# A decoder's first self-attention layer: merging its weighted values by DMA through DRAM instead of by transposes on TensorE

## The reference

```python
def proj(w, b):
    y = jnp.einsum('bsd,ed->bse', x, w) + b
    return y.reshape(B, S, N_HEADS, HEAD_DIM).transpose(0, 2, 1, 3)
q = rope(proj(wq, bq)); k = rope(proj(wk, bk)); v = proj(wv, bv)
score = jnp.einsum('bhqd,bhkd->bhqk', q, k) / math.sqrt(HEAD_DIM)
score = jnp.where(causal[None, None], score, -jnp.inf)
attn = jax.nn.softmax(score, axis=-1)
out = jnp.einsum('bhqk,bhkd->bhqd', attn, v)
out = out.transpose(0, 2, 1, 3).reshape(B, S, DIM)
return jnp.einsum('bsd,ed->bse', out, wo) + bo
```

## Time and profile before

| | |
|---|---|
| Median of three executions | 828.93 us (827.77 to 837.93) |
| The profiled execution | 833.08 us, its span 831.0 us |
| Mean granted TensorE clock | 0.898 |
| TensorE busy over the span | 677.5 us (82%) |
| DVE, ACT, POOL busy | 589.4, 413.5, 284.0 us |
| Moved by DMA | 71.27 MB, mean 86 GB/s |
| Chain that ended last, by engine | PE 60%, DVE 18%, issue 8%, POOL 5%, ACT 4%, DMA 4% |

### The profile page before, as it was taken

One profiled execution on the slowest core, in us unless ns is written; L12 is line 12 of the kernel. 1 busy time (PEld: TensorE's weight loads), 2 busy tenths in 40 slices (PEclk: granted clock), 3 DMA queues, 4 the chain that ended last, 5 costly groups with the idle time before them and its releaser, 6 DMA issues.

```text
span 831.0 us, 14947 instructions
## 1 busy us (share of the span) xinstructions
PE 677.5 (82%) x4693; PEld 330.3 (40%) x4698; DVE 589.4 (71%) x1606; ACT 413.5 (50%) x708; POOL 284.0 (34%) x504
## 2 busy tenths in 40 slices
PE   2759999999988885099999933687999989897987
PEld 1335454444445443056666622122332323323543
DVE  3757778777647776567878845688889898953564
ACT  1332565655666552023333312156788777785544
POOL 4742454445542146612323210213232142341310
PEclk9875999999989987589999985578999999999899
DMA  7452655484232315211111133221224111000000
GB/s 222 148 182 99 203 160 164 123 230 141 84 87 73 99 44 166 71 36 40 42 43 40 42 112 108 73 85 44 82 73 128 31 48 52 2 2 1 13 14 26
DMA packets 74780, 71.27 MB, mean 86 GB/s; under 512 B 14560, under 2 KB 67168, under 8 KB 74704
## 3 DMA queue, kind: packets, MB, share of 16 engines
q1 hardware_dynamic: 72000, 64.84, 25.9%
q0 software_dynamic: 2272, 4.69, 1.8%
q10 hardware_dynamic: 432, 0.79, 0.3%
HBM read 41.90 MB, written 28.00 MB: 84 GB/s over the span
## 4 chain that ended last, share of the span: by engine, by line
PE 60%; DVE 18%; issue 8%; POOL 5%; ACT 4%; DMA 4%; SPq 1%; DVEq 0%; POOLq 0%; ACTq 0%
PE bank_pv L733 10%; DVE mx L591 9%; PE bank_turn L575 8%; PE bank_scores L2025 5%; PE bank_scores L1775 4%; PE bank_turn L1760 4%; PE bank_scores L685 4%; PE bank_scores L1760 4%; POOL routed_tokens L1727 2%; PE bank_turn L752 2%; PE bank_scores L1768 2%; PE bank_turn L528 1%; DMA stk<-stack_A 1%; PE bank_turn L579 1%; DVE stats L450 1%
## 5 line engine op out<-in xcount | busy, mean ns | idle before, releaser
L591 DVE TENSOR_REDUCE mx<-bank_turn 128x1 f32<-128x512 f32 (+3 forms) x452 | 260.7, 616 | 63.2 <-PE bank_turn L580 33.3
L575 PE MATMUL bank_turn<-stk 64*128 64x128 bf16 (+3 forms) x708 | 167.0, 318 | 29.4 <-DVE mx L591 19.8
L685 PE MATMUL bank_scores<-stk 64*128 64x512 bf16 (+4 forms) x576 | 173.6, 364 | 4.6 <-ACT probs L706 3.6
L710 ACT ACTIVATE probs<-bank_scores 128x1024 f32<-128x1024 f32 (+4 forms) x160 | 117.3, 768 | 102.9 <-PE bank_scores L685 102.5
L706 ACT ACTIVATE probs<-bank_scores 128x512 f32<-128x512 f32 x256 | 138.6, 606 | 35.7 <-PE bank_scores L685 34.7
L733 PE MATMUL bank_pv<-probs,vsl 128*32 128x512 f32 (+4 forms) x1152 | 138.9, 555 | 2.6 <-POOL probs L718 1.7
L575 PEld LDWEIGHTS bank_turn<-stk 64*128 64x128 bf16 x708 | 57.4, 99 | 132.5 <-DVE mx L591 63.6
L718 POOL TENSOR_SCALAR_AFFINE_SELECT probs<-probs 128x256 f32<-128x256 f32 x128 | 51.8, 408 | 75.4 <-ACT probs L710 74.1
L1743 POOL DMA_INDIRECT expert_outputs<-probs,y_at x39 | 37.3, 957 | 101.4 <-DVE probs L1662 98.4
L1807 ACT COPY okT<-bank_scores 128x512 f32<-128x512 f32 x39 | 22.9, 586 | 81.3 <-PE bank_scores L1768 81.3
L477 POOL TENSOR_TENSOR rstd<-var,mhalf 128x4 f32<-128x4 f32 x24 | 25.4, 1056 | 110.8 <-DVE var L456 110.6
(11 more groups left out here) (299 smaller groups left out, 1137.3 us busy)
## 6 DMA issues: line engine op xcount, KB each, us to landing
stk<-stack_A SPq DMA_DIRECT2D x64, 256.0 KB, 3.2
w<-in_M_w SPq DMA_DIRECT2D x12, 512.0 KB, 4.8
stack_A<-parts SPq DMA_DIRECT2D x15, 384.0 KB, 3.2
stack_A<-fill SPq DMA_DIRECT2D x8, 512.0 KB, 5.8
stk<-stack_X SPq DMA_DIRECT2D x16, 256.0 KB, 2.7
stack_A<-parts SPq DMA_DIRECT2D x15, 256.0 KB, 3.3
probs<-routed_tokens SPq DMA_DIRECT2D x39, 65.0 KB, 1.8
b_gated<-in_M_b SPq DMA_DIRECT2D x1, 2048.0 KB, 11.6
```

The source lines that it names most:

```text
L575: mm = e.matmul(o, stk[r, slot, 0, pp, qt * P:(qt + 1) * P], stk[r, slot, 1, pp, 0:keys], start=True, stop=not a.causal)
L591: e.tensor_reduce(o.rearrange("p h q -> p q h"), bank_of((g, m))[:, 0:k * wide].rearrange("p (q h k) -> p q h k", q=len(tiles), h=len(hs)) ...
L685: mm = e.matmul(score_bank(g, kt, i)[0:a.kp, 0:S - q0], stk[r, slot, 1, pp, kt * P:kt * P + a.kp], stk[r, slot, 0, pp, q0:S], start=True, ...
L710: e.activation(probs[0:a.kp, probs_of(g, kt), j:HG:2, 0:n], bank_scores[0:a.kp, 2 * j:2 * j + 2, 0:n], ACT.Exp, scale=1 / math.sqrt(HD)).t ...
```

## The change

For the 16 units of A0 (the list `SENT`) the finish and the merge on TensorE, DVE and ACT are gone. In their place:

- `keep_sp`: in unit g, between the load and the shift, SP sends unit g - 1's four rows of sums to `sums_in` (128 partitions of 16) and then all of `oT` to DRAM (256 KB).
- `reciprocal_dve`: in the third chunk of units 4, 8 and 12 (in unit 16 at its end, ahead of the copy of the turned maxima) DVE waits for the sums of four units and takes the reciprocals, 128x64.
- `rec_out_sp` and `merge_sp`: last in that unit's list, SP sends the reciprocals to DRAM, reads the weighted values of all 16 heads into `okT` (256 KB), waits until the reciprocals have landed, and reads them replicated 8 times into `rec_all` (256 KB).
- `merge_pool`: in the second chunk of unit 4b + 5, after its masks, POOL waits for both and multiplies; for the last batch at the end of unit 17.
- The projection waits for that; for the first three batches it is moved from the first to the fourth chunk of unit 4b + 5. For the last batch it stays in unit 18.
- The bias of the values is added to the values (`values_pool`) in all three layers, and no longer at the merge.

X0 and A1 keep their finish and merge on TensorE. The diff, cut to its core:

```diff
@@
+SENT = list(range(NB))
+TURNED = [u for u in range(3 * UN) if u // UNITS not in SENT]
...
+def merged_in(g):
+
+    u = g - (3 if X0.first <= g - 1 < A1.first else 2)
+    u = u if u % UNITS == UNITS - 1 else -1
+    return u if u >= 0 and sent(u) and last_of_stream(u) == last_of_stream(g) else None
+
+
+def reciprocal_in(g):
+
+    return g - 1 if g and g % UNITS == 0 and sent(g - 1) and last_of_stream(g - 1) == last_of_stream(g) else None
...
-        w |= {(4 * b + 4, "c"): ("merge", A0, b), (4 * b + 5, "a"): ("proj", A0, b),
+        w |= {(4 * b + 5, "c"): ("proj", A0, b),
...
-    w |= {(18, "a"): ("merge", A0, 3), (18, "b"): ("proj", A0, 3), (21, "a"): ("turn", X0, 3), (21, "b"): ("q", X0, 3)}
+    w |= {(18, "b"): ("proj", A0, 3), (21, "a"): ("turn", X0, 3), (21, "b"): ("q", X0, 3)}
...
-                i = e.tensor_copy(vsl[:, slot, :, :, 0:HD],
-                                  vraw[:, QT * b:QT * (b + 1), slot * HG * HD:(slot + 1) * HG * HD]
-                                  .rearrange("p t (h d) -> p t h d", h=HG))
+                i = e.tensor_tensor(vsl[:, slot, :, :, 0:HD],
+                                    vraw[:, QT * b:QT * (b + 1), slot * HG * HD:(slot + 1) * HG * HD]
+                                    .rearrange("p t (h d) -> p t h d", h=HG),
+                                    bias.rearrange("p (h d) -> p h d", h=HG).unsqueeze(1).to_broadcast([P, QT, HG, HD]),
+                                    ALU.add)
...
             if g > 1:
-                e.wait_ge(*filled(("finish", g - 2)))
+                if sent(g - 2):
+                    e.wait_ge(s["sums"][(g - 2) % UNITS], 16 * (sends_at(g - 2) + 1))
+                    e.wait_ge(s["kept"][(g - 2) % UNITS], 16 * (sends_at(g - 2) + 1))
+                else:
+                    e.wait_ge(*filled(("finish", g - 2)))
             e.copy(oT[:, g % 2], bank_pv[:]).then_inc(s["pv_out"], 1)
+
+        def keep_sp(e, g):
+
+            k, hg = sends_at(g), g % UNITS
+            e.wait_ge(s["pv_out"], g + 1)
+            wait(e, s["recips"], k)
+            e.dma_start(sums_in[:, hg], oT[HD:P:VW, g % 2, :]).then_inc(s["sums"][hg], 16)
+            wait(e, s["merged"], k - 1)
+            e.dma_start(scr_o[k % 2, hg], oT[:, g % 2, :]).then_inc(s["kept"][hg], 16)
+
+        def reciprocal_dve(e, g):
+            k = sends_at(g)
+            for hg in range(UNITS):
+                e.wait_ge(s["sums"][hg], 16 * (k + 1))
+            wait(e, s["rec_out"], 16 * k)
+            e.reciprocal(recs[:], sums_in[:]).then_inc(s["recips"], 1)
+
+        def rec_out_sp(e, g):
+            k = sends_at(g)
+            e.wait_ge(s["recips"], k + 1)
+            wait(e, s["merged"], k - 1)
+            e.dma_start(scr_r[k % 2].rearrange("(g h) (b n) -> (h b) g n", g=UNITS, b=P // HG), recs[:])\
+                .then_inc(s["rec_out"], 16)
+
+        def merge_sp(e, g):
+
+            k, of = sends_at(g), g // UNITS
+            if of:
+                e.wait_ge(*filled(("proj", of - 1)))
+            for hg in range(UNITS):
+                e.wait_ge(s["kept"][hg], 16 * (k + 1))
+            e.dma_start(okT[:], scr_o[k % 2].rearrange("g (h r) n -> (g h) r n", h=HG)[:, 0:HD, :]).then_inc(s["raw_in"], 16)
+            e.wait_ge(s["rec_out"], 16 * (k + 1))
+            wait(e, s["merged"], k)
+            e.dma_start(rec_all[:], scr_r[k % 2].unsqueeze(1).to_broadcast([NH, HD, S])).then_inc(s["rep_in"], 16)
+
+        def merge_pool(e, g):
+            k = sends_at(g)
+            e.wait_ge(s["raw_in"], 16 * (k + 1))
+            e.wait_ge(s["rep_in"], 16 * (k + 1))
+            e.tensor_tensor(okT[:], okT[:], rec_all[:], ALU.mult).then_inc(s["merged"], 1)
...
                         if c == 2 and u is not None:
                             finish_dve(e, u)
+                        if c == 2 and reciprocal_in(g) is not None:
+                            reciprocal_dve(e, reciprocal_in(g))
...
                 if a.kt > 1:
+                    if c == 1 and merged_in(g) is not None:
+                        merge_pool(e, merged_in(g))
                     beside_pool(e, g, c)
...
                 load_sp(e, g + ahead)
+            if g not in (STREAMS[0].start, STREAMS[1].start) and sent(g - 1):
+                keep_sp(e, g - 1)
             if layer(g) is not X0:
                 for t in turned_in(g):
                     shift_sp(e, t)
...
             if g == W_PIECES:
                 parts_out_sp(e)
+            if reciprocal_in(g) is not None:
+                rec_out_sp(e, reciprocal_in(g))
+                merge_sp(e, reciprocal_in(g))
```

More of the change, by code:

```diff
@@ L267, in build @@
         s = {n: sem(f"att_{n}") for n in """up_in up_dve up_act part1 rest part2 part3 roped
-            stacked_q stacked_k values neg_hi neg scores probs masked pv pv_out reciprocal biased""".split()}
+            stacked_q stacked_k values neg_hi neg scores probs masked pv pv_out reciprocal recips rec_out
+            rep_in raw_in merged biased""".split()}
         s["filled"] = [sem(f"filled{i}") for i in range(TURNS)]
@@ L272, in build @@
         s["shifted"] = [sem(f"shifted{i}") for i in range(UNITS)]
+        s["sums"] = [sem(f"sums{i}") for i in range(UNITS)]
+        s["kept"] = [sem(f"kept{i}") for i in range(UNITS)]
         chunk0 = [chunk_at(g) for g in range(3 * UN + 1)]
@@ L651, in values_pool @@
                 e.wait_ge(s["pv"], chunk0[g - UNITS + 1])
+            if g == a.first:
+                if a is A0:
+                    e.wait_ge(s_out_w, 16 * len(out_loads))
+                elif a is X0:
+                    e.wait_ge(s_soon, 16 * len(soon))
+                else:
+                    e.wait_ge(s_later, 16 * len(later))
+            bias = wts[a.name]["bv"][:, slot * HG * HD:(slot + 1) * HG * HD]
             if a is X0:
                 e.wait_ge(*emptied(("v", X0.ln, 0)))
[L654 to L655 removed]
+                i = e.tensor_tensor(vsl[0:SC, slot, 0, :, 0:HD],
+                                    vx[0:SC, b, slot * HG * HD:(slot + 1) * HG * HD].rearrange("p (h d) -> p h d", h=HG),
+                                    bias[0:SC].rearrange("p (h d) -> p h d", h=HG), ALU.add)
             else:
                 value_wait(e, a, b)
[L658 to L660 removed]
+                i = e.tensor_tensor(vsl[:, slot, :, :, 0:HD],
[3 more added lines that the diff above has]
+                                    ALU.add)
             i.then_inc(s["values"], 1)
@@ L755, in finish_dve @@
         def finish_dve(e, g):
-            hg, of = g % UNITS, g // UNITS
+            hg, of, n = g % UNITS, g // UNITS, TURNED.index(g)
             e.wait_ge(*filled(("finish", g)))
-            if g:
-                e.wait_ge(*emptied(("finish", g - 1)))
+            if n:
+                e.wait_ge(*emptied(("finish", TURNED[n - 1])))
             src = bank_of(("finish", g))[:].rearrange("p (q h c) -> p q h c", q=QT, h=HG)
             e.reciprocal(rec[:], src[:, :, :, HD]).then_inc(s["reciprocal"], 1)
-            e.wait_ge(s["reciprocal"], g + 1)
-            if hg == 0 and of > 1:
+            e.wait_ge(s["reciprocal"], n + 1)
+            if hg == 0 and n >= 2 * UNITS:
                 e.wait_ge(*filled(("merge", of - 2)))
@@ L774, in merge_pe @@
             for j in range(QT):
[L775 removed]
+                i = e.transpose(bank[:, j * P:(j + 1) * P], otok[:, of % 2, j, :], ident[:])
             i.then_inc(is_filled(("merge", of)), 1)
@@ L780, in merge_act @@
             e.wait_ge(*filled(("merge", of)))
-            if of:
-                e.wait_ge(*filled(("proj", of - 1)))
-            e.activation(okT[:], bank_of(("merge", of))[:], ACT.Identity, bias=wts[a.name]["bv"][:])\
-                .then_inc(is_emptied(("merge", of)), 1)
+            e.wait_ge(*filled(("proj", of - 1)))
+            e.copy(okT[:], bank_of(("merge", of))[:]).then_inc(is_emptied(("merge", of)), 1)
         def proj_pe(e, a, b, part):
@@ L788, in proj_pe @@
             if part == 0:
-                e.wait_ge(*emptied(("merge", of)))
+                if of in SENT:
+                    e.wait_ge(s["merged"], SENT.index(of) + 1)
+                else:
+                    e.wait_ge(*emptied(("merge", of)))
                 take_bank(e, ("proj", of), out=OPEN)
@@ L1143, in unit_pool @@
             if a.kt == 1:
+                if merged_in(g + 1) is not None:
+                    merge_pool(e, merged_in(g + 1))
                 for step in range(4):
@@ L2217, in on_all @@
             return row.to_broadcast([P, D])
-        def column(row):
-            return row.rearrange("o p -> p o")
         def loads_of(a, names):
```

22 lines of the change are left out of this document (14 added, 8 removed).

## The result

The changed kernel took 842.11 us (median of 4 runs, 837.18 to 845.89) beside 831.91 us for the kernel before (4 runs, 827.77 to 837.93): ratio 1.0109, interval 1.0059 to 1.0159. Measured again with more runs it took 841.21 us (12 runs) against 835.86 us (35 runs): ratio 1.0060, interval 1.0024 to 1.0096. So the change costs 5 us or a little more, inside 2%, but with the other sign than the 1.3 us that I forecast to be gained. One thing must be known to read all that follows: executions of the same kernel lie up to 18 us apart (827 to 845 us for the one before), the longer ones at a lower mean granted clock (0.904 at 828.73 us, 0.880 at 845.50). The first three runs of before had the median 828.93; with 19 to 35 runs it was 834.84 to 835.92.

The account below looks back on a forecast made before the run. TensorE's chain was taken to bound the first self-attention layer. Gain 12.0 less losses 1.5 + 0.5 + 4.7 + 4.0 = 10.7 left 1.3 us: 833.08 to 831.8 us profiled, 827.6 beside the median 828.93; range 815 to 843.

Parts of the forecast that it names:

- The gain: First layer: fifteen finishes 8.9 us and three merges 1.8 us leave TensorE, 1.3 us leaves DVE; 12.0 us gained.
- that rival: Transposes on TensorE are worth their whole duration: 23.0 us would go, time 805 to 815 us; chance 0.05.
- DVE did not take over either: Rival: DVE's maxima end last once finishes go, little gained while losses stay, up to 840 us; chance 0.10.
- The sums and the bias: DVE waits for sums in units 4, 8, 12, 0.5 us each, 1.5 us lost; value bias on POOL costs nothing.
- The merge of unit 5: Merge inputs there 13 to 16 us after unit 4's load, covered; 0.5 us allowed in all for the full queue.
- The 2048 KB transfer: Issued in unit 9, delays load and shift behind it: 3.2 us more wait, 1.5 us clock, 4.7 lost (0 to 7).
- The crossing: Units 16 to 19, into cross-attention: the last batch's merge comes late on a bare path, 4.0 us lost (2.6 to 5.6).
- The all-covered rival: Second queue position, merge chain and crossing all hide: 15.3 us gained, 817.8 us, about 814 in the median's terms; chance 0.14.

Follow-up runs that it names:

- early_merge: Changed kernel with the merge transfers issued ahead of the unit's fills, constants and expert weights, no byte more or less: 838.11 us, ratio 1.0032 to before.
- the two queue kernels: weights_moved and early_merge, both the changed kernel with other transfers no longer ahead of the reciprocals' write: 837.11 and 838.11 us.
- s_none: Changed kernel with no batch sent by DMA, only the value bias on GpSimd left: 838.57 us, ratio 0.9971 to before.
- early_pieces: early_merge with the 2048 KB bias in four pieces of 512 KB in units 12 to 15, all batches by DMA: 832.75 us, ratio 0.9949 to before.
- kept_only: Old transposes and merge, with the sums and kept 256 KB per unit also sent but read by nobody, bias on GpSimd: 840.93 us, ratio 1.0041 to before.
- the kernels with batch 0 or 3 alone: Changed kernel with only that batch by DMA, the others by transposes: batch 0 844.28 us, ratio 1.0112; batch 3 846.13 us, ratio 1.0140 to before.
- the kernel before in pieces: Kernel before with only its 2048 KB bias split into four pieces of 512 KB in units 12 to 15: 836.14 us, ratio 0.9998 to before.
- weights_moved: Changed kernel with unit 4's constant fill moved to unit 6 and its expert weights to unit 13: 837.11 us, ratio 1.0004 to before.

## Why the prediction was wrong

**The gain: right.** 12.0 us forecast. Measured: 0.66 to 0.69 us per finish, about 10.2 for fifteen; units 4, 8 and 12 became 2.02 to 2.16 us shorter, of which some 0.68 is the finish, and the rest the merge and the projection that moved on into the next unit. With 0.6 to 0.7 per merge that is about 12.2. The Trainium skill's 275 ns for a transpose ("TensorE: Matmul & The Clock Gate", Part 4) would have shortened a unit by 1.1 us, an estimate; it did not, and that rival falls. DVE did not take over either: TensorE's waits for the maxima are 3.1 us from 116 to 262 us in both kernels, and early_merge had gained 6.1 us by unit 9.

**The sums and the bias: too dear and right.** 1.5 us for DVE's wait in units 4, 8 and 12 was 0 (idle 0.0 ahead of L807).

**The merge of unit 5: the step that failed.** I wrote that the inputs are there 13 to 16 us after the load of unit 4, against a mask at 18.6 (9.8 to the next load and 8.8 more), "covered", and allowed 0.5 us. After a load issued at 112.58 the inputs came at 130.72, 18.1 us. The write was issued 10.7 us after that load in place of 8.5, because seven issues in 4.96 us stood between the shift and it, not five of 0.5; it landed in 4.14 us where my upper end was 3.5. The seven could be read in the trace of before, where they take 118.65 to 122.75 us (the first line has three of them):

```profile
118.65 1.53 SPq L909 DMA_DIRECT2D stack_kx<-parts  x3
120.22 0.46 SPq L1172 DMA_DIRECT2D stack_A<-fill  x1
120.72 0.54 SPq L1174 DMA_DIRECT2D gate_w<-in_M_gate_w  x1
121.30 0.94 SPq L1174 DMA_DIRECT2D gate_b<-in_M_gate_b  x1
122.29 0.46 SPq L2258 DMA_DIRECT2D w<-in_M_w  x1
```

And GpSimd was ready at 126.77, 14.2 us after the load, where by the rows of before its idle stretch runs from 16.8 to 18.6 us: the units that the change had shortened reached the wait sooner, while I had taken the deadline from the kernel before. The late inputs alone would have held the mask up by some 0.8 us (18.1 and 1.3 for the multiplication, against 18.6; an estimate); the gain itself ate the rest of the cover, and the lower clock stretched what followed. Without a wait unit 5 takes some 9.6 us (before's 9.20 less a finish, and the projection's 0.9 to 1.2 that units 9 and 13 show when nothing waits); it took 15.69. The term is 6 us, 3.9 of it wait, not 0.5, and the two queue kernels take 4.9 and 5.5 us of it back in their profiles, 3 to 4 us in their medians. Unit 9, which I had called covered as well, adds 0.5 us in one profile and about 4 in the other.

**The 2048 KB transfer: mechanism right, size open between 2.8 and 5.8 us.** Forecast 4.7 us more (3.2 of wait and 1.5 of clock). The wait grew by 4.0, units 10 and 11 by 4.4 on top of two finishes saved, 5.8. Two rows from executions that differ by chance are behind this: s_none alone waits 2.80, and beside its units 10 and 11 the growth is 1.4 us, 2.8 with the two finishes. From early_merge to early_pieces, which differ in the pieces alone, these units go from 25.9 to 20.7 us, and the medians differ by 5.4 us, the ratios by 0.8%. But a layer at its old pace runs into the transfer too: s_none, kept_only and the kernels with batch 0 or 3 alone take 26.3 to 27.0 us for the two units, the kernel before in pieces 21.5.

**The crossing: right.** Forecast 4.0 (2.6 to 5.6); units 16 to 18 grew by 4.4, and leaving batch 3 out gives 2.6 (ratios) to 4.9 us (medians). The profiles scatter: 18.9 to 21.9 us with the whole merge of batch 3 through DRAM, 14.6 to 17.8 without.

So with measured terms: -12.2, 0.9 for the three projections' new place (1.0 each where they stand now, 0.7 saved where they stood), 6.1, 0.5, 5.8 and 4.4 give +5.5 us where I had -1.3. The copy of unit 18 lies 6.4 us later than before's, both counted from the first copy. Against s_none it lies only 3.1 us later, since there 3.0 us more go to the 2048 KB transfer without the change. So up to that copy the change costs 3 to 6 us. The profile's remaining 3.3 us are the low clock of units 23 to 30 (+6.9) less what the stretches behind it gave back. That this is scatter is likely, since the kernel before in pieces has it too, but that the change has no part in it is not shown. The all-covered rival failed by the same three stalls.

## What to carry to other kernels

When a change shortens the engine on the path, redo every deadline with the shortened units: a chain of transfers that hangs on one queue's order doesn't come sooner with it. Count all issues ahead of a chained transfer, and put the links of a chain ahead of transfers that nobody waits for yet; here that order alone took unit 5 from 15.7 to 10.8 us and some 3 us, hardly more than the scatter, from the time, and with the large transfer cut up and the bare crossing left as it was, a change that had cost 0.6 to 1.1% gained 0.8%. Before trusting a difference of two profiles, look at the same units in a kernel where they are unchanged.

## What the hardware showed that was not expected

A write of only 32 KB took as long as whole tiles: the reciprocals landed in 2.5 us at the crossing (248.32 to the next issue at 250.82) and in 4.14 us behind unit 4's queue, the 256 KB of weighted values in 2.2 us (median of 15). Most of that is not the write itself. The trace has its packets, 512 of 64 bytes: of the write issued at 123.24 the first starts at 126.12 and the last at 126.78, of the one at 248.32 at 249.80 and 250.30; in both, packets of transfers issued ahead (4096 bytes of expert weights, 1024 of the stack) run until just before or into them. "DMA: Bandwidth & Descriptors" of the Trainium skill, Specifications, puts the least transfer for the line rate at 512 bytes. The 0.5 to 0.7 us that these packets take don't settle it, and no run here changed the size of the pieces.

An idle stretch of 3.9 us on TensorE was followed by a granted clock of 0.50 for about 6 us of full work (133 to 139 us); with no wait at that place (early_merge) the clock stayed at 1.00. Yet weights_moved, whose waits were 0.70 and 0.78 us, had a clock of 0.50 at 136 to 138 us too. And in early_merge a wait of 1.16 us on TensorE, at 132.60, had no fall behind it, so that the length of a wait alone doesn't decide. This second part of a stall's price does not show as a wait, and the traces here don't say how short a stall escapes it.
